# Transposes of the maxima's parts, and their copy, one slot later in each quarter step of a vision-tower layer

## The reference, cut to what matters

```python
h = _L0_tok_ref(0, x, W0, W1, Wo)                    # relu(x W0) * (x W1), then Wo
h = concatenate([cls_tok, h], axis=1)                # 513 rows
h = h + _L0_attn_ref(_layernorm(h), w_q, w_k, w_v, w_o)
h = h + _L0_ffn_ref(_layernorm(h), gate_w, gate_up_w, down_w)

# inside _L0_attn_ref, for each image and each of the 16 heads
scores = einsum('bhqd,bhkd->bhqk', q, k) * SCALE
attn = softmax(scores, axis=-1)
out = einsum('bhqk,bhkd->bhqd', attn, v)
```

## Time and profile before

| | |
|---|---|
| median of 3 executions | 2339.58 us (2336.57 to 2345.38) |
| the profiled execution | 2333.89 us, its span 2331.8 us |
| TensorE busy | 2018.2 us, 87% of the span, mean granted clock 0.952 |
| VectorE busy | 1602.1 us, 69% |
| ScalarE busy | 1236.2 us, 53% |
| GpSimd busy | 915.8 us, 39% |

### The profile page before, as it was taken

How to read it: one execution, slowest core, us unless ns; L and a number is a source line. 1 busy time by engine, 2 the same in 40 slices (tenths; PEclk the granted TensorE clock), 3 DMA queues, 4 the chain that set the end, 5 groups by cost and what they waited for, 6 DMA issues and landing times. The chain is left out here.

```text
span 2331.8 us, 49727 instructions
## 1 busy us (share of the span) xinstructions
PE 2018.2 (87%) x13328; PEld 1154.2 (49%) x13329; DVE 1602.1 (69%) x4268; ACT 1236.2 (53%) x2600; POOL 915.8 (39%) x894
## 2 busy tenths in 40 slices
PE   4789999898998998989899898885129999999997
PEld 2333443343443444444344443222128988888885
DVE  4477888887887888888788889883274444444443
ACT  0246566565665655656556566563054545544553
POOL 2222233423333244232342334333136666666653
PEclk9899999999999999999999999897559999999999
DMA  2312323222223223222232222210244433333331
GB/s 88 100 58 67 96 73 86 80 78 70 83 78 84 74 69 90 72 83 81 63 88 73 84 77 78 69 43 28 100 154 66 64 63 63 62 63 62 63 58 22
DMA packets 171884, 172.27 MB, mean 74 GB/s; under 512 B 30787, under 2 KB 160405, under 8 KB 171669
## 3 DMA queue, kind: packets, MB, share of 16 engines
q1 hardware_dynamic: 141396, 134.87, 20.2%
q0 software_dynamic: 30272, 34.80, 9.3%
HBM read 100.70 MB, written 68.99 MB: 73 GB/s over the span
## 5 line engine op out<-in xcount | busy, mean ns | idle before, releaser
L1157 DVE TENSOR_REDUCE mxs<-bank 128x1 f32<-128x512 f32 x1024 | 696.8, 684 | 199.2 <-PE bank L502 175.6
L832 ACT ACTIVATE pt<-bank 128x512 f32<-128x512 f32 x1024 | 589.1, 594 | 377.0 <-PE bank L511 374.3
L502 PE MATMUL bank<-ks,qs 96*128 96x512 bf16 x1024 | 399.9, 392 | 88.4 <-DVE mxs L1157 69.8
L511 PE MATMUL bank<-qs,ks 99*128 99x512 bf16 x1024 | 395.0, 387 | 9.9 <-ACT pt L832 9.4
L1775 PE MATMUL bank<-xh,gu_h 128*128 128x256 bf16 (+1 forms) x1152 | 309.4, 269 | 3.6 <-issue 1.9
L1775 PE MATMUL bank<-xl,gu_h 128*128 128x256 bf16 (+1 forms) x1152 | 308.3, 268 | 0.0
L1775 PE MATMUL bank<-xh,gu_l 128*128 128x256 bf16 (+1 forms) x1152 | 308.2, 268 | 0.0
L1735 POOL DMA_INDIRECT out<-y_sb,ids x136 | 217.3, 1597 | 202.8 <-ACT y_sb L1826 182.2
L502 PEld LDWEIGHTS bank<-ks,qs 96*128 96x128 bf16 x1024 | 103.4, 101 | 358.2 <-DVE mxs L1157 246.1
L520 PE MATMUL bank<-pt,v_sb 128*32 128x512 f32 x2048 | 278.4, 616 | 0.0
L1883 DVE TENSOR_TENSOR hid_e<-bank,act_g 128x256 f32<-128x256 f32 (+1 forms) x288 | 117.0, 406 | 169.7 <-PE bank L1775 166.5
(11 more groups left out here) (290 smaller groups left out, 3466.2 us busy)
## 6 DMA issues: line engine op xcount, KB each, us to landing
qs<-qk_dram SPq DMA_DIRECT2D x128, 128.0 KB, 2.6
ks<-qk_dram SPq DMA_DIRECT2D x64, 192.0 KB, 3.4
xt<-x_t SPq DMA_DIRECT2D x16, 512.0 KB, 4.2
h_dram<-h_sb SPq DMA_DIRECT2D x16, 512.0 KB, 3.7
qs<-qk_dram SPq DMA_DIRECT2D x128, 64.0 KB, 2.3
ks<-qk_dram SPq DMA_DIRECT2D x64, 128.0 KB, 3.3
hw<-h_dram SPq DMA_DIRECT2D x16, 512.0 KB, 4.4
out<-hw SPq DMA_DIRECT2D x16, 512.0 KB, 3.0
```

The source lines that it names most:

```text
L502: mm(score[u % 2][:, :], qs[0:QK, h, blk(t)], ks[0:QK, h, :], start=True, stop=True) \
L511: mm(scoret[u % 2][:, :], ks[0:QK + MROWS, h, blk(t)], qs[0:QK + MROWS, h, :], start=True, stop=True).then_inc(s("pe_st"), 1)
L832: f(pt[:, t % 2, j, :], scoret[u % 2][:, :], ACT.Exp).then_inc(s("act_exp"), 1)
L1157: v.reduce_max(mxs[:, t, g * GH + j:g * GH + j + 1], score[u % 2][:, :], AX.X).then_inc(s("dve_mx"), 1)
```

## The change

TensorE's four transposes and ScalarE's copy are each placed one slot later; their waits, SP's, VectorE's and GpSimd's programs stay as they are.

```diff
--- before.py
+++ after.py
@@ -643,7 +643,7 @@
                         for t in range(TB):
                             last = tr(d2[:, blk(t)], pvs[:, blk(t)], identf)
                         last.then_inc(s("pe_tg"), 1)
-                    if u == 9 and mt[0].ok:
+                    if u == 10 and mt[0].ok:
                         b, gg = mt
                         wait(pe, s("dve_nm"), NG, b, gg + 1)
                         if tg[0].ok:
@@ -852,7 +852,7 @@
                         b, gg = mt
                         wait(act, s("dve_dsc"), NG, b, gg + 1)
                         f(pcls[:, b.par, :, heads(gg)], dsc[:, :, heads(gg)], ACT.Exp).then_inc(s("act_pcls"), 1)
-                    if u == 10 and mt[0].ok:
+                    if u == 11 and mt[0].ok:
                         b, gg = mt
                         wait(act, s("pe_mt"), NG, b, gg + 1)
 
```

## The result

| | before | after |
|---|---|---|
| median of 8 executions each, same chip | 2340.18 us (2334.36 to 2345.38) | 2352.03 us (2341.57 to 2355.62) |
| ratio after / before, 95% interval | | 1.005 (1.0033 to 1.0066) |
| the profiled execution | 2333.89 us, span 2331.8 | 2341.57 us, span 2339.6 |
| mean granted clock of TensorE in it | 0.952 | 0.948 |

The change costs 0.5%, some 12 us by the medians. The profiled execution of after is the fastest of its eight, and that of before is faster than all eight of its own; the two traces lie 7.7 us apart. The forecast was no visible change, 2337.1 us; the time lies above its range.

A forecast was written before the change was run, and what follows sets the result against it. TensorE is busiest (87%), but VectorE bounds the third and fourth quarters, TensorE the second, neither the first. Fourth quarter 2.3 plus unloaded ends 0.2 gives 2.5 us less: 2339.58 - 2.5 = 2337.1 us, no visible change, range 2327 to 2346.

The forecast's parts named there:

- Third quarter ... Worth 0: Slots 9 to 13: the 0.68 us stall goes, TensorE waits about 1.4 us for VectorE's maximum instead; gain 0.
- Second quarter and first quarter: Second: TensorE's busy stretch ends the same, at most 0.1 us; first: sums of slot 10 wait for VectorE's residual; gain 0.
- Fourth quarter: Slot 10's maximum 0.33 us sooner, swallowed in nine of sixteen steps by waits for GpSimd; 7 x 0.33 = 2.3 us gain.
- The later copy and DMA: Cost nothing: copy 0.25 us ahead of x2's transposes in the second quarter, DMA 1.5 us to spare in the fourth.
- Rival A: The stall before the transposes is worth its full length: 19.4 us faster, 2320.2 us; chance 0.10.
- Rival B: Second quarter's x2 transposes in slot 12 wait for the later copy: 13.1 us slower, 2352.7 us; chance 0.06.
- Rival C: VectorE's four-column products meet GpSimd differently in eight of sixteen steps: 13.2 us, to 2326.4 or 2352.8 us; chance 0.04.
- Its argument against: GpSimd's work beside the long four-column product is started by VectorE's own product, so both keep their distance.

The follow-up runs named there:

- Kernels 1: Kernel before with transposes and copy each one slot later in the third quarter only; 2347.41 us, ratio to before 1.0045.
- kernel 2: Kernel before with transposes and copy each one slot later in all quarters but the third; 2336.51 us, ratio to before 0.9993.
- kernel 8: Kernel before with only the third quarter's v product of slot 11 put behind slot 12's score products; 2350.68 us, ratio to before 1.0044.
- kernel 5: Kernel before with only ScalarE's copy one slot later, transposes in their old slot; 2341.05 us, ratio to before 1.0012.
- kernel 11: Changed kernel with the router's last piece (`picked`) in slot 40 instead of 41, `wts` left in slot 42; 2327.31 us, ratio to before 0.9984.
- kernel 3: Changed kernel plus six unused 512-column products in TensorE's idle time at slot 12 of the third quarter; 2371.15 us, ratio to before 1.0126.

## Why the prediction was wrong, point by point

**The step that failed** is "Third quarter ... Worth 0". Its first half was right: the stall ahead of the transposes went, TensorE came earlier to the wait for the maxima, and the wait took up what was saved (forecast about 1.4 us from 0.75 + 0.68, and 1.43 us found in the steps with the long `wts`, of which the forecast had read one; in steps with the long `picked` it is 1.75 us from 0.72 + 1.01, or 2.28 from 0.68 + 1.62; in the whole run 69.8 to 77.6 us, forecast about 80). The conclusion that the same idle time in one piece costs the same as in two was wrong. Kernels 1, 2, 8, the table behind kernel 8 and the rows of the clock show it: behind the longer wait TensorE runs part of the f32 products at the 1.2 GHz level, and since the quarter has VectorE as its bound and TensorE has to feed it within a slot, the loss, about 1.4 us a step, is passed on in full. It was 11.1 us in the eight steps of the profiled execution. The forecast priced the place of idle time at nothing, without a reason, and looked at one of the two kinds of step only; all eight steps are of the other kind. The trace of before had the material: its step 11, shown above, has this very fall after a wait of 1.62 us, ahead of the same products.

**Second quarter and first quarter: worth 0.** Right within the 0.1 us that was allowed: the second quarter costs 0.07 us per step, about 1 us in all, and kernel 2 shows nothing.

**Fourth quarter: 0.33 us sooner, lost where TensorE waits for GpSimd's quantized output.** The gain was there, 0.48 us per step. It was lost earlier than forecast, and in nearly all steps: in slot 15, where VectorE's four-column instruction runs longer beside GpSimd's pass. What I called independent of the maxima (GpSimd's chain) was independent; that is why VectorE met it. The term of the sum was -2.3 us; found are -0.48 + 0.42 = -0.06 us per step, some -1 us for all sixteen. The count of steps behind the term was misread, too: the nine waits of the earlier trace rows are waits and not steps, seven at the start of a step and two in the emptying end of the phase.

**The later copy and DMA: nothing.** Right within 0.12%; the margin of 0.25 us forecast for the second quarter was a little too wide, since x2's weight loads wait 0.2 us for the copy in ten steps.

**Rival A** (the full 19.4 us) did not happen. The rule quoted for it from the Trainium skill, page "Perfetto Trace Analysis", section "Optimization Strategy", is not borne out: the gap ahead of the transposes on the most-used engine was removed, and the kernel is 0.5% slower. **Rival B** got the sign and nearly the size (2352.7) by a mechanism of which kernel 5 shows 0.12% at most; a right number from a wrong cause, which is luck. **Rival C** is there, as the smaller part. Its size was 8 steps of 1.65 us; found are three more of twelve steps with the long `picked` in place of the long `wts`, worth 1.0 to 1.1 us each rather than 1.65, because either way one piece is long and only its place changes. Its argument against is true as far as it goes: in steps 3 to 12 GpSimd starts its class part 0.49 us behind VectorE's product in both kinds of step. But the distance does not decide. L1251 starts 0.02 to 0.03 us behind GpSimd in either kind, and lasts 0.18 or 0.65 us. What happened is rival C together with an effect that no rival has: the long `picked` makes a wait, and that wait, merged with the other, lowers the clock.

The Trainium skill, page "SBUF — State Buffer", section "Who interferes with whom", says that a VectorE instruction with two SBUF inputs contends with GpSimd's reads. The runs agree for `picked` (0.19 or 2.06 us) and `wts` (0.16 or 1.81 us), and kernel 11 shows the same for a tensor-scalar instruction (0.16 or 1.85 us at L1265), which the argument of the prediction had not counted among them.

**What stays open.** Which of VectorE and GpSimd gets through first when L1251 and L1000 start within 0.03 us, and whether the change shifts that or only the execution does; how the 0.5% divides between transposes and copy; and the profile's 7.7 us against 12 us of the medians, of which the trace of the fastest execution can tell nothing. The share of the clock is 11.1 us of gross loss in one trace. That the merged wait makes falls more frequent is shown with the meetings held fixed (the table behind kernel 8); its price in time was not measured apart from them, because kernel 3, meant for that, changed other things.

## What to carry to other kernels

A wait that is taken from an engine which then waits for the same slower engine is not always free: look at how long the merged wait is, what TensorE runs right behind it, and whether that work feeds the engine that is the bound. Look in the trace of before for places where the granted clock fell, and ask whether the change makes more of them. Where steps come in two kinds, read the waits in both. And where a median of 0.16 us stands beside a maximum of 1.8 us, move that instruction out of the other engine's pass before tuning the order around it: two small router instructions in another slot were worth 1.0% on the kernel before, and with them moved the change cost nothing.

## What the runs showed of the hardware

- TensorE's granted clock, 1.00 in a stretch in which it is busy 6.61 of 9.00 us with its idle time in short pieces, fell to the 1.2 GHz level in 21 of 24 steps behind one idle of 1.75 to 2.28 us with one of up to 0.58 us behind it, in 4 of 23 where the first stood in two pieces, and once behind one of 1.05 us that had no fall behind it in the other trace: 512-column bf16 products went from 0.22 to 0.40 us apart, eight f32 products from 1.89 to 3.06 us. In steps 2 to 13 of after no score product from slot 48 to the step's end was slow.
- A VectorE instruction on 4 or 32 columns that reads SBUF and starts beside GpSimd's pass of 2.13 us ended within 0.05 us of it: L1256 (0.19 us otherwise) lasted 2.06 us, L1267 (0.16) 1.81 us, L1265 (0.16) 1.85 us. L1227 went from 0.46 to 0.87 us beside GpSimd's shorter instructions.
- When two such instructions started within 0.03 us of each other, either could give way: L1251 lasted 0.65 us beside 0.63 us of GpSimd's L1000, or 0.18 us beside 0.70 us, with the same 0.02 to 0.03 us between their starts.
- Six added products per step in one phase went with 20 us more of TensorE's "issue" idle in another phase that was left as it was (kernel 3). No run here tells why.
